# Cross attentions of a two-layer decoder: softmax denominators as (head, chunk) rows and a block product

## The reference, cut to what matters

```python
q = (query @ Wq + bq).reshape(B, Sq, H, hd)
k = (key @ Wk + bk).reshape(B, Sk, H, hd)
v = (value @ Wv + bv).reshape(B, Sk, H, hd)
score = jnp.einsum('bqhd,bkhd->bhqk', q, k)
cmask = jnp.triu(jnp.ones((Sq, Sk), dtype=bool), k=1)
score = jnp.where(cmask, -jnp.inf, score)
att = jax.nn.softmax(score * scale, axis=-1)
ret = jnp.einsum('bhqk,bkhd->bqhd', att, v).reshape(B, Sq, D)
return ret @ Wo + bo
```

## Time and profile before

| what | us |
|---|---|
| runs, median of 3 (lowest, highest) | 1463.44 (1462.82, 1471.08) |
| the profiled execution's own time | 1454.73 |
| its span, first to last instruction | 1452.9 |
| PE busy in the span | 1224.3 |
| DVE busy in the span | 1003.2 |
| ACT busy in the span | 728.7 |

### The profile page before, as it was taken

One profiled execution on the slowest core, in us unless ns is written; L12 is line 12 of the kernel. 1 busy time (PEld: TensorE's weight loads), 2 busy tenths in 40 slices (PEclk: granted clock), 3 DMA queues, 4 the chain that ended last, 5 costly groups with the idle time before them and its releaser, 6 DMA issues.

```text
span 1452.9 us, 46525 instructions
## 1 busy us (share of the span) xinstructions
PE 1224.3 (84%) x19382; PEld 773.1 (53%) x19382; DVE 1003.2 (69%) x2562; ACT 728.7 (50%) x1815; POOL 232.5 (16%) x200
## 2 busy tenths in 40 slices
PE   5889898797689999898985889888987898889775
PEld 3343434295367666666662357634763476346564
DVE  4577676645677877877763588588858785878542
ACT  1323141453367666766741449443944395439543
POOL 2011121142030131031011030003000400030044
PEclk9999999899999999999997899999999999999888
DMA  8900000022340100101004000000000000060021
GB/s 306 332 17 1 18 1 8 10 58 88 116 162 4 28 24 5 33 19 36 7 7 103 11 1 2 4 5 11 3 4 1 16 2 2 1 161 3 1 83 46
DMA packets 61024, 63.21 MB, mean 44 GB/s; under 512 B 27756, under 2 KB 51569, under 8 KB 59664
## 3 DMA queue, kind: packets, MB, share of 16 engines
q1 hardware_dynamic: 55184, 51.68, 12.0%
q0 software_dynamic: 2752, 5.29, 1.1%
q10 hardware_dynamic: 2880, 3.28, 0.6%
HBM read 32.58 MB, written 28.55 MB: 42 GB/s over the span
## 4 chain that ended last, share of the span: by engine, by line
PE 56%; DVE 20%; ACT 12%; issue 7%; DMA 2%; POOL 1%; ACTq 1%; SPq 1%; POOLq 0%; DVEq 0%
PE ps L1208 5%; PE ps L1218 5%; DVE arena L639 5%; PE ps L1653 4%; PE ps L1234 4%; ACT arena L1744 3%; PE ps L510 3%; DVE arena L1808 3%; PE ps L536 3%; PE ps L1258 2%; PE ps L1708 2%; ACT arena L1754 2%; DVE arena L1818 2%; ACT arena L1328 2%; PE ps L1699 2%
## 5 line engine op out<-in xcount | busy, mean ns | idle before, releaser
L1371 DVE TENSOR_REDUCE nmax<-ps 128x1 f32<-128x512 f32 x256 | 166.6, 682 | 56.9 <-PE ps L1218 56.5
L1744 ACT ACTIVATE arena<-ps,arena 128x512 f32<-128x512 f32 (+3 forms) x256 | 134.6, 539 | 73.3 <-DVE arena L1808 70.2
L1328 ACT ACTIVATE arena<-ps,nmax 128x512 f32<-128x512 f32 x172 | 118.8, 694 | 67.9 <-DVE nmax L1371 67.2
L1808 DVE TENSOR_REDUCE arena<-ps 128x1 f32<-128x512 f32 (+3 forms) x256 | 115.6, 484 | 13.2 <-PE ps L1668 11.6
L639 DVE TENSOR_REDUCE arena<-ps 128x8 f32<-128x1232 f32 x64 | 89.1, 1437 | 27.8 <-PE ps L498 27.5
L1379 DVE COPY arena<-ps 128x512 f32<-128x512 f32 x128 | 87.2, 681 | 24.0 <-PE ps L1234 24.0
L274 PE MATMUL ps<-identb 128*128 128x512 bf16 x306 | 83.4, 412 | 23.7 <-DVE rows L936 7.7
L1818 DVE TENSOR_SCALAR arena<-arena 128x512 f32<-128x512 f32 (+3 forms) x256 | 92.0, 391 | 5.7
L1754 ACT COPY arena<-ps 128x512 f32<-128x512 f32 x160 | 85.8, 596 | 12.5 <-PE ps L1683 12.5
L1683 PE MATMUL ps<-sqc,arena 64*128 64x64 f32 x1280 | 66.9, 234 | 24.5 <-ACT arena L1754 12.1
L1699 PE MATMUL ps<-arena 128*64 128x128 f32 x1280 | 87.5, 279 | 0.0
(11 more groups left out here) (360 smaller groups left out, 2553.8 us busy)
## 6 DMA issues: line engine op xcount, KB each, us to landing
xs_d<-onehot SPq DMA_DIRECT2D x3, 2704.0 KB, 28.1
gs_d<-kmask SPq DMA_DIRECT2D x8, 645.0 KB, 10.1
cw<-in_cw SPq DMA_DIRECT2D x2, 2048.0 KB, 11.9
rv<-in_rv SPq DMA_DIRECT2D x2, 1536.0 KB, 16.9
late<-in_gw SPq DMA_DIRECT2D x3, 1024.0 KB, 10.0
arena<-gs_d SPq DMA_DIRECT2D x23, 129.0 KB, 2.1
xs_d<-onehot SPq DMA_DIRECT2D x1, 2288.0 KB, 20.9
onehot<-q_s SPq DMA_DIRECT2D x96, 8.0 KB
```

The costliest lines, as they stand in the source:

```text
L1328: nc.scalar.activation(PB[k % 6], ps[:, k % 5, :], ACT.Exp, bias=nmax[:, u:u + 1], accum_out=rsum[:, b % 2, u:u + 1]).then_inc(SD["exp"], 1)
L1371: nc.vector.tensor_reduce(nmax[:, k % NU:k % NU + 1], ps[:, k % 5, :], AX.X, ALU.max, negate=True)\
L1744: ins = nc.scalar.activation(TF["p%d" % (n % 2)][:, h * S + c0:h * S + c1], ps[:, FSB[n % 2][h], c0:c1], ACT.Exp, bias=TF["nmax"][:, k8:k8 ...
L1808: ins = nc.vector.tensor_reduce(TF["nmax"][:, k8:k8 + 1], ps[:, FSB[n % 2][h], c0:c1], AX.X, ALU.max, negate=True)
```

## The change: what it does

`sums` multiplies 64 columns at a time: chunk n (64 queries) of group g goes through a weight `vchunk[:, z, n]` that sends head h's sum to output row 8h + n only. All chunks add into the same 128 x 64 of bank 6, so the denominators are a 128 x 64 tile with rows (head, chunk). DVE takes one reciprocal of it into `acc0`, and makes `r`, 128 x 512, by two products (4 chunks each) with `part8`, which is one where a row's chunk is that column block. PE multiplies each half of `r` with the constant `block` (one where two rows belong to one head), which spreads each head's reciprocals over its 8 dimensions (`spread`, into banks 6 and 1, 256 columns each). ACT copies the values out of PSUM into the first `pt` tile, since DVE's product now reads the spread reciprocals from PSUM. `spread` is put behind `pe_warm` in PE's list. The constants `part8`, `same8` and `vchunk` are made once, in `dve_prepare`. Semaphore counts follow.

```diff
@@ -127,6 +127,9 @@
         sel = sb("sel", [P, NPER, P], BF16)
         xmaskT = sb("xmaskT", [P, NPER, KP], BF16)
         kcol = sb("kcol", [P, B, NPER])
+        same8 = sb("same8", [P, DK, DK])
+        part8 = sb("part8", [P, DK])
+        vchunk = sb("vchunk", [P, 2, DK, GR])
         pcol = sb("pcol", [P, NPER])
         mt = sb("mt", [P, NT, P], BF16)
         mT = sb("mT", [P, S], BF16)
@@ -227,7 +230,10 @@
         NXP, XV, XS = 7, 7, 6
         XEXP = [(n, 1 + (n % NG4 == 1 and n % NXP < NXP - 1)) for n in range(NPER * NG4)
                 if n % NG4 != 2 or n % NXP == 0]
-        NXE = len(XEXP)
+        NXE = len(XEXP) + 1
+        XCH, XCW = DK, S // DK
+        NXO = NT + 2
+        XRB = (XS, 1)
         xexp = lambda n: 1 + max(m for m, (n0, _) in enumerate(XEXP) if n0 <= n)
 
 
@@ -540,15 +546,24 @@
 
             def sums():
                 for j in (0, NPER - 1):
-                    for g in range(NG4):
-                        if j == 0:
-                            pe.wait_ge(s["acc"], both(k, b) * NACC + NACC - NG4 + g + 1)
-                        else:
-                            pe.wait_ge(s["exp"], both(k, b) * NXE + xexp(NG4 * j + g))
-                        ins = nc.tensor.matmul(ps[GR * g:GR * (g + 1), XS, :], vmask[:, j, :],
-                                         TX[f"pt{j % 2}{g}"] if j else TX[f"acc{g}"], start=(j == 0), stop=(j == NPER - 1),
-                                         skip_group_check=True, tile_position=(0, GR * g))
+                    for n in range(XCH):
+                        chunk = slice(n * XCW, (n + 1) * XCW)
+                        for g in range(NG4):
+                            if j == 0 and n == 0:
+                                pe.wait_ge(s["acc"], both(k, b) * NACC + NACC - NG4 + g + 1)
+                            elif n == 0:
+                                pe.wait_ge(s["exp"], both(k, b) * NXE + xexp(NG4 * j + g))
+                            ins = nc.tensor.matmul(ps[GR * g:GR * (g + 1), XS, 0:XCW], vchunk[:, j // (NPER - 1), n, :],
+                                                   (TX[f"pt{j % 2}{g}"] if j else TX[f"acc{g}"])[:, chunk],
+                                                   start=(j == 0 and n == 0), stop=(j == NPER - 1 and n == XCH - 1),
+                                                   skip_group_check=True, tile_position=(0, GR * g))
                 ins.then_inc(s["sum"], 1)
+
+            def spread():
+                for z in range(2):
+                    pe.wait_ge(s["o"], both(k, b) * NXO + z + 1)
+                    nc.tensor.matmul(ps[:, XRB[z], 0:256], c["block"], TX["r"][:, z * 256:z * 256 + 256],
+                                     start=True, stop=True).then_inc(s["sum"], 1)
 
             for n in range(NXH):
                 if k == "E" and b and n == 1:
@@ -577,8 +592,9 @@
                 pe_G_rank(pe, b - 1)
             pe_bias(DH[k][0], 1, k + "_bo")
             pe_warm(4, 0)
+            spread()
             for i in range(NT):
-                pe.wait_ge(s["o"], both(k, b) * NT + i + 1)
+                pe.wait_ge(s["o"], both(k, b) * NXO + 2 + i + 1)
                 nc.tensor.matmul(ps[:, OB[DH[k][0], 1], i * P:(i + 1) * P], aoT[:, i * P:(i + 1) * P], w[k + "_o"],
                                  start=False, stop=True, skip_group_check=True).then_inc(SH[DH[k][0]]["wo"], 1)
 
@@ -613,6 +629,8 @@
                 act.wait_ge(s["st"], both(k, b) * NPER * NG4 + n + many)
                 nc.scalar.activation(PTX[j % 2][:, g:g + many, :], ps[:, n % NXP:n % NXP + many, :], ACT.Exp, scale=scale,
                                      bias=kcol[:, b, j:j + 1] if k == "B" else pcol[:, j:j + 1]).then_inc(s["exp"], 1)
+            act.wait_ge(s["pv"], both(k, b) * NPER + NPER)
+            nc.scalar.copy(PTX[0][:, 0, :], ps[:, XV, :]).then_inc(s["exp"], 1)
 
         def dve_X_values(dve, b, k):
             s = XA[k]
@@ -652,17 +670,19 @@
                         dve.wait_ge(s["acc"], both(k, b) * NACC + NG4 * (j - 2) + g + 1)
                     nc.vector.tensor_tensor(TX[f"acc{g}"], TX[f"pt{j % 2}{g}"], TX[f"acc{g}" if j > 1 else f"pt0{g}"], ALU.add)\
                         .then_inc(s["acc"], 1)
-            dve.wait_ge(s["sum"], both(k, b) + 1)
-            r = TX["r"]
-            part = [slice(i * P, (i + 1) * P) for i in range(NT)]
-            landed = [ch.mark(nc.vector.reciprocal(r[:, part[0]], ps[:, XS, part[0]]))]
+            dve.wait_ge(s["sum"], both(k, b) * 3 + 1)
+            r = TX["r"].rearrange("p (n w) -> p n w", n=XCH)
+            ch(nc.vector.reciprocal(TX["acc0"][:, 0:XCW], ps[:, XS, 0:XCW]))
+            for z in range(2):
+                n4 = slice(4 * z, 4 * z + 4)
+                nc.vector.tensor_tensor(r[:, n4, :], TX["acc0"][:, 0:XCW].unsqueeze(1).to_broadcast([P, 4, XCW]),
+                                        part8[:, n4].unsqueeze(2).to_broadcast([P, 4, XCW]), ALU.mult).then_inc(s["o"], 1)
+            dve.wait_ge(s["exp"], both(k, b) * NXE + NXE)
             for i in range(NT):
-                if i + 1 < NT:
-                    landed.append(ch.mark(nc.vector.reciprocal(r[:, part[i + 1]], ps[:, XS, part[i + 1]])))
-                ch.wait(landed[i])
-                if i == 0:
-                    dve.wait_ge(s["pv"], both(k, b) * NPER + NPER)
-                nc.vector.tensor_tensor(aoT[:, part[i]], ps[:, XV, part[i]], r[:, part[i]], ALU.mult).then_inc(s["o"], 1)
+                part = slice(i * P, (i + 1) * P)
+                if i % 2 == 0:
+                    dve.wait_ge(s["sum"], both(k, b) * 3 + 2 + i // 2)
+                nc.vector.tensor_tensor(aoT[:, part], ps[:, XRB[i // 2], i % 2 * P:i % 2 * P + P], PTX[0][:, 0, part], ALU.mult).then_inc(s["o"], 1)
             if k == "B":
                 ph = DH[k][0]
                 dve.wait_ge(SH[ph]["wo"], b * NWO[ph] * NT + 2 * NT)
@@ -792,6 +812,14 @@
             nc.vector.tensor_reduce(pcol[:, :], vmask[:, :, :], AX.X, ALU.max).then_inc(s_prep, 1)
             dve.wait_ge(s_prep, 4)
             nc.vector.tensor_scalar(pcol[:, :], pcol[:, :], 1.0, -MASKED, ALU.subtract, ALU.mult).then_inc(s_prep, 1)
+            index8 = row["index"][:, 0:DK]
+            nc.vector.tensor_reduce(part8[:, :], c["ident"].rearrange("p (g d) -> p d g", d=DK), AX.X, ALU.add)
+            ch(nc.vector.tensor_tensor(same8[:, :, :], index8.unsqueeze(2).to_broadcast([P, DK, DK]),
+                                       index8.unsqueeze(1).to_broadcast([P, DK, DK]), ALU.is_equal))
+            for z, j in enumerate((0, NPER - 1)):
+                ch(nc.vector.tensor_tensor(vchunk[:, z, :, :].rearrange("p n (h d) -> p n h d", h=HG),
+                                           vmask[:, j, :].rearrange("p (h d) -> p h d", h=HG).unsqueeze(1).to_broadcast([P, DK, HG, DK]),
+                                           same8[:, :, :].unsqueeze(2).to_broadcast([P, DK, HG, DK]), ALU.mult))
             ch(nc.vector.tensor_reduce(tmp[:, 0:GR], c["ident"].rearrange("p (g k) -> p k g", k=GR), AX.X, ALU.add))
             nc.vector.tensor_copy(repeat[:, :].rearrange("p (h k) -> p h k", h=HG), tmp[:, 0:GR].unsqueeze(1).to_broadcast([P, HG, GR]))\
                 .then_inc(s_flipped, 1)
```

## The result

| | before | after |
|---|---|---|
| median of the runs, us (lowest to highest, number) | 1461.24 (1449.96 to 1471.08, 20) | 1469.24 (1464.18 to 1477.09, 20) |
| profiled execution, its span, us | 1454.73, 1452.9 | 1470.63, 1468.7 |

The ratio is 1.0056, 95% interval 1.0037 to 1.0074: the change costs 8.2 us (5.4 to 10.8). That lies within 1%, and 1469.24 within the range, but the forecast was +1.4 us. The two profiled executions are 15.9 us apart, more than the runs are; a cause is sought for the 8.2. All ratios here leave out executions that took over 1.5% longer than the fastest of the same kernel.

What follows compares the result with a forecast made beforehand. PE's in-order queue, not DVE, was taken to bound the cross-attention tails. Five at +0.1 and three at +0.3 us, the rest hidden, gave +1.4 us: 1456.1 profiled, 1464.8 on the median of 1463.44; range 1457 to 1473.

Steps and rivals of the forecast that it cites:

- What bounds the tail: Cross-attention tail: PE's in-order queue holds the spread behind bias and warm-ups; +0.1 us per attention, +0.3 with the ranks.
- Rival (b): Cross-attention tail: follows DVE, PE taking the spread once r is ready; 1.5 us gained each, 1451.5 us in all; chance 0.03.
- The sums: Denominator sums on PE: 64 narrow matmuls replace 8 wide ones, 14.4 ns a pass; +0.03 us at most per attention.
- rival (a): Denominator sums bound by weight loads: +2.6 us per attention, 1485.5 us, or 1472.3 at the lower price; chance 0.06.
- DVE: Cross-attention tail: one reciprocal and two products, 1.45 us, replace four reciprocals, 3.75 us; DVE falls by 2.3 us per attention.
- The products: DVE's output products behind the spread: 0.23 us each, a pair 0.15 apart, done in 0.42 us.
- The copy and the set-up: ACT's copy of the values (0.58 us) and DVE's extra preparation in the first attention (1.5 us once): both hidden.
- The test named in the prediction: First attention's preparation: mask copies ending after 38 us would show the forecast wrong.
- rival (c): Half-clock stretches change length, each worth at most 3.4 us either way; eight give 1457 to 1472; chance 0.13.
- 8 matmuls of 512 columns become 64 of 64: the same 4096 columns: Denominator sums on PE: column count unchanged, with 128 passes in place of 16.

Runs made afterwards that it cites:

- before + 160: The kernel before plus 80 short matmuls (160 TensorE instructions) ahead of the self-attention stage; ratio 1.0078, and 1.0039 when run again.
- after + 96: The changed kernel plus 48 short matmuls (96 TensorE instructions) ahead of the self-attention stage; ratio 1.0023, and 1.0009 when run again.

## Why the prediction was right, and where it was not

- **What bounds the tail.** Right: PE's in-order queue, not DVE. The spread starts 2.68 us after the reciprocal directly behind the warm-ups (forecast 2.7), and with the ranks 2.88, from 1276.76 to 1279.64 in the last attention (forecast 2.9). Taking the warm-ups away moved it to 1.80, which is what shows that the queue held it. Rival (b), the tail that follows DVE, did not occur; with the warm-ups gone 0.53 of its 1.5 us a tail appeared (0.32 to 0.35 with the ranks).
- **The sums.** Right, and rival (a) falls. PE's loads, up to the last exponential and behind it:

```profile
73.53 0.95 PEld L556 LDWEIGHTS ps<-arena,vchunk 128*32 128x32 f32 x64 [0.25 <-DVE arena L671]
...
74.77 0.87 PEld L556 LDWEIGHTS ps<-arena,vchunk 128*32 128x32 f32 x57 [0.29 <-ACT arena L630]
```

  64 loads in 0.95 us are 15 ns a pass, as taken from line 1258 in the earlier trace rows. The Trainium skill's "TensorE: Matmul & The Clock Gate", Part 3, lets a load hide behind a running matmul only in another row group. The trace doesn't agree: here all tiles share it, and a round of four takes 60 ns, not the 230 of tiles in turn.
- **DVE.** Right: one reciprocal of 0.56 (forecast 0.55) and two products of 0.42, by the groups (line, operation, count, busy us, mean ns):

```profile
L685 DVE TENSOR_TENSOR aoT<-ps,arena 128x128 f32<-128x128 f32 x32 | 7.1, 283 | 16.8 <-PE ps L565 16.8
...
L678 DVE TENSOR_TENSOR arena<-arena,part 128x256 f32<-128x256 f32 x16 | 6.1, 423 | 0.3
...
L675 DVE RECIPROCAL arena<-ps 128x64 f32<-128x64 f32 x8 | 4.5, 560 | 18.7 <-PE ps L556 18.7
```

  Its busy time fell by 15.7 us and not by some 18: that figure left out the set-up (1.5 us) and the dearer products of the next point (32 x 0.055 = 1.8 us).

- **The products.** A term mis-sized. The step "products of 0.23, a pair 0.15 apart" took L665's two in 0.42; the new ones take 0.283 each, four in 0.88. The form is the same, a factor from PSUM and one from SBUF; why it takes longer wasn't tried. The kernel before had both prices for this form: beside L665's 0.228 its line 439 took 0.282. The projection's start came 3.73 us after the reciprocal (forecast 3.6), and with the sums' 0.05 this is the +0.24 in place of +0.1, and +0.43 to +0.45 in place of +0.3: +2.5 us over eight, not +1.4.
- **The copy and the set-up.** Hidden, as said. ACT's timeline: the copy ends at 77.35, and DVE wants it at 79.28.

```profile
76.76 0.59 ACT L633 COPY arena<-ps 128x512 f32<-128x512 f32 x1 [2.04 <-PE ps L542]
77.36 1.28 ACT L343 ACT_TABLE_LOAD   x1
```

  In the preparation DVE still idles 1.91 us ahead of the mask copies (2.03 in the earlier trace rows), so the added instructions lay in an idle time. The test named in the prediction, copies that end after 38 us, was a bad one: they end later because PE's masks came later. In after PE stood still for 0.73 us without a semaphore in the middle of them, until 35.39, and many of the later passes took 0.29 us in place of 0.23.

```profile
38.49 0.29 DVE L791 CAST sel<-ps 128x128 bf16<-128x128 f32 x1 [1.91 <-PE ps L775]
```

- **The clock**, rival (c). Not the cause: 0.943 and 0.944 over the runs, and 0.941, 0.946 and 0.947 in before + 160, after + 96 and the changed kernel without warm-ups. The stage that lengthened has 6.8 us at half clock in the trace of before and 3.4 in that of after, so the clock would have shortened it.
- **The step that failed.** "8 matmuls of 512 columns become 64 of 64: the same 4096 columns" priced the matmuls where they run, and priced 1,856 more instructions at nothing. Where they run that was right to 0.05 us. But they arrive in packets of 256, and 928 of them ahead of stage D moved all its borders by 160. The runs show that this shift alone, without the change, costs 0.4 to 0.8%, and that putting the borders back takes the changed kernel to 1.0009 and 1.0023. The prediction had no term and no rival for it. That the time still fell within 1% is because the shift costs no more, and that 1469.24 lies within 1457 to 1473 is luck: the upper end was set for the clock and for slow loads, and neither came. Which border costs how much, how the 6 us divide over the stages, and whether the waits at the borders make up all of it stays open.

## What to carry to other kernels

Before moving work from one engine to another, look at what stands in the receiving engine's queue ahead of it: the saving of DVE was worth nothing until four idle-looking warm-ups went. Count the instructions that an edit adds, as well as the columns: where a later stage streams short passes, a changed count moves the borders of its code, and here it moved the time by some 0.3 to 0.8%. So for an effect of that size, run a control padded to the same count modulo 256 before crediting or blaming the edit.

## What the runs showed of the hardware that was not expected

PE can be held up by its own code. In stage D it stood still with no semaphore to wait for, at the borders between code packets and nowhere else for over 0.4 us: 15 times in the given profile (14.3 us together), 16 times in that of after (16.5 us), ending 1.2 to 1.6 us after a q8 packet had landed. The expectations' 25 and 31 us of such stalls are not what these waits add up to. The long ones near 416 us fall where transfers keep the DMA engines busy: 99% of the time from 411.5 to 415.9 us in the given profile, all of it from 416 to 419.9 and from 421.5 to 425.7 in that of after; no run moved these transfers. The Trainium skill, "Runtime: NRT & Kernel Launch", section on instruction fetch mechanics, says that code is refilled in blocks of 16 KiB, 256 instructions, and that crossing one is mostly hidden. The size agrees with 16.4 KB a packet; "mostly hidden" doesn't agree with these waits, in a stage that has passes 14 ns apart.

Narrow matmuls over four column tiles with a new weight each cost nearly the same as wide ones where they run: 64 of them took 0.05 us longer than 8 with the same number of columns.
